# Two column strips for the band mask, two diagonal tiles for the causal mask

## What is computed

```python
def band_attention(q, k, v, mask):       # four layers
    # query chunks of W = 64 attend to 3W keys (prev/current/next chunk), band-masked
    scores = einsum('bhcqd,bhckd->bhcqk', qc, kb) / sqrt(d)
    rel = arange(3 * W)[None, :] - W - arange(W)[:, None]
    band_ok = abs(rel) <= W
    allowed = mb & pos_ok & band_ok
    scores = where(allowed, scores, -1e9)
    probs = softmax(scores)
...
def _L0_attn_ref(x, ...):                # one layer, after a layer norm
    att = einsum('bhqd,bhkd->bhqk', q, k) * D ** (-0.5)
    att = where(tril(ones((T, T))), att, -inf)
    att = softmax(att)
```

## Time and profile before

| | |
|---|---|
| median of 3 runs | 5886.05 us (5884.61 to 5886.73) |
| the profiled execution | 5917.47 us, its span 5915.7 us |
| PE busy | 5233.6 us, 88% |
| PE weight loads busy | 4004.3 us, 68% |
| DVE busy | 3505.7 us, 59% |
| ACT busy | 2533.2 us, 43% |
| POOL busy | 1121.5 us, 19% |

### The profile page before, as it was taken

One profiled execution on the slowest core, in us unless ns is written; L12 is line 12 of the kernel. 1 busy time (PEld: TensorE's weight loads), 2 busy tenths in 40 slices (PEclk: granted clock), 3 DMA queues, 4 the chain that ended last, 5 costly groups with the idle time before them and its releaser, 6 DMA issues. The chain is left out here.

```text
span 5915.7 us, 122499 instructions
## 1 busy us (share of the span) xinstructions
PE 5233.6 (88%) x43730; PEld 4004.3 (68%) x43730; DVE 3505.7 (59%) x8938; ACT 2533.2 (43%) x4800; POOL 1121.5 (19%) x1056
## 2 busy tenths in 40 slices
PE   0799998999999899999999999699999822899999
PEld 0577776777777677777777777466666622676666
DVE  6566665566666566666566666477777567222222
ACT  0355554455554455555455555255555500111111
POOL 5111111111111111111111111000000002333343
PEclk9999999999999999999999999899999956899999
DMA  6544444544444544444444444344434300323332
GB/s 100 110 87 94 88 91 78 97 96 85 94 87 85 97 84 97 84 97 85 87 95 84 97 83 88 72 88 88 90 86 93 69 9 4 93 63 78 83 81 41
DMA packets 1283995, 488.99 MB, mean 83 GB/s; under 512 B 1086531, under 2 KB 1270560, under 8 KB 1283872
## 3 DMA queue, kind: packets, MB, share of 16 engines
q1 hardware_dynamic: 1256224, 450.68, 36.0%
q0 software_dynamic: 27648, 36.72, 4.0%
HBM read 162.87 MB, written 60.28 MB: 38 GB/s over the span
## 5 line engine op out<-in xcount | busy, mean ns | idle before, releaser
L757 ACT ACTIVATE pT<-banks 128x384 f32<-128x384 f32 x1920 | 924.9, 491 | 663.6 <-PE banks L522 662.8
L965 DVE TENSOR_REDUCE mx<-banks 128x4 f32<-128x768 f32 x768 | 719.3, 950 | 304.6 <-PE banks L504 304.6
L1147 POOL TENSOR_TENSOR rstd<-ve,half 128x2 f32<-128x2 f32 x288 | 218.9, 760 | 3240.9 <-DVE ve L874 3240.9
L612 PE MATMUL banks<-nT,w 64*128 64x256 f32 x5760 | 754.2, 394 | 21.7 <-DMA b<-in_b 2.9
L502 PE MATMUL banks<-maskb,eyeb 128*128 128x384 bf16 x1920 | 633.9, 330 | 52.4 <-DMA qkT<-stack 25.2
L612 PEld LDWEIGHTS banks<-nT,w 64*128 64x128 f32 x5760 | 515.7, 187 | 191.8 <-PE banks L612 79.1
L504 PE MATMUL banks<-qkT 128*128 128x192 bf16 (+2 forms) x3840 | 634.5, 247 | 0.0
L522 PE MATMUL banks<-qkT 128*128 128x192 bf16 (+2 forms) x3840 | 633.9, 247 | 0.0
L625 PE MATMUL banks<-w,pT 128*128 128x192 f32 x3072 | 554.5, 330 | 0.0
L625 PEld LDWEIGHTS banks<-w,pT 128*128 128x128 f32 x3072 | 492.7, 190 | 42.4 <-issue 21.9
L520 PE MATMUL banks<-mseq,eyeb 128*128 128x384 bf16 x1536 | 502.7, 327 | 18.2 <-DMA qkT<-mrT 14.8
(11 more groups left out here) (200 smaller groups left out, 8602.3 us busy)
## 6 DMA issues: line engine op xcount, KB each, us to landing
hcur<-hbuf SPq DMA_DIRECT2D x164, 192.0 KB, 2.6
resid<-hbuf SPq DMA_DIRECT2D x160, 192.0 KB, 2.5
amb<-am_d SPq DMA_DIRECT2D x130, 192.0 KB, 3.1
hbuf<-hout SPq DMA_DIRECT2D x128, 192.0 KB, 2.0
exp_wg<-in_ewg SPq DMA_DIRECT2D x16, 768.0 KB
exp_wu<-in_ewu SPq DMA_DIRECT2D x16, 768.0 KB
exp_wd<-in_ewd SPq DMA_DIRECT2D x16, 576.0 KB
xs<-xr SPq DMA_DIRECT2D x32, 272.0 KB, 2.2
```

The source lines that it names most:

```text
L612: last = nc.tensor.matmul(up_bank(s, f), w1[rows, c, up_cols(ph, f)], nT[s][rows, c, :], start=(step == 0), stop=(step == 2))
L757: ph.inc(nc.scalar.activation(pT[s][:, h % NPT, :], bank[s][h % 2][:, 0:SCOLS], ACT.Exp, scale=SCALE), "p", s)
L965: last = nc.vector.tensor_reduce(mx[s][:, :, at].rearrange("p t h -> p h t"), src[:, :, 0:SCOLS].rearrange("p h (t k) -> p h t k", t=T), A ...
```

## The change

In the banded layers the mask is written by two matmuls. The first takes the identity's columns 0 to 63 and writes rows 0 to 63 of the bank, columns 64 to 383; the second takes the identity's columns 64 to 127 and writes rows 64 to 127, columns 0 to 319. Both are placed by `tile_position`, at column 0 and column 64 of the array, and the program gives them a 128 x 64 tile. What is left out (row below 64 with column below 64, row from 64 on with column from 320 on) holds no closed entry. In the causal layer one matmul writes columns 0 to 127 and 256 to 383 (a stepped output and a stepped mask operand), 256 columns in place of 384. The score matmuls still accumulate on what the mask wrote and overwrite the rest. `stop=True` and `skip_group_check=True` on them change no operation.

```diff
+        def pe_masks(ph, dst, mask):
+            if ph is tok:
+                nc.tensor.matmul(dst[0:D64, D64:SCOLS], eyeb[:, 0:D64], mask[:, D64:SCOLS], start=True, stop=True,
+                                 tile_position=(0, 0))
+                nc.tensor.matmul(dst[D64:P, 0:SCOLS - D64], eyeb[:, D64:P], mask[:, 0:SCOLS - D64], start=True,
+                                 stop=True, tile_position=(0, D64))
+            else:
+                ends = lambda x: x[:, 0:SCOLS].rearrange("p (x c) -> p x c", c=P)[:, 0:3:2, :]
+                nc.tensor.matmul(ends(dst), eyeb[:], ends(mask), start=True, stop=True)
...
-            nc.tensor.matmul(dst[:, 0:SCOLS], eyeb[:], maskb[:, masks, :], start=True, stop=False)
+            pe_masks(ph, dst, maskb[:, masks, :])
             for t, (c0, f0, w) in enumerate(qcols):
                 last = nc.tensor.matmul(dst[:, c0:c0 + w], qT[s][:, h, t * P:(t + 1) * P],
-                                        kT[s][:, h, f0:f0 + w], start=False, stop=(t == T - 1))
+                                        kT[s][:, h, f0:f0 + w], start=False, stop=True, skip_group_check=True)
...
-            nc.tensor.matmul(dst[:, 0:SCOLS], eyeb[:], mseq[s][:] if ph is tok else maskb[:, 3, :], start=True, stop=False)
+            pe_masks(ph, dst, mseq[s] if ph is tok else maskb[:, 3, :])
```

More of the change, by code:

```diff
@@ L519, in pe_scores2 @@
             dst = bank[s][h % 2]
-            nc.tensor.matmul(dst[:, 0:SCOLS], eyeb[:], mseq[s][:] if ph is tok else maskb[:, 3, :], start=True, stop=False)
+            pe_masks(ph, dst, mseq[s] if ph is tok else maskb[:, 3, :])
             for t, (c0, f0, w) in enumerate(kcols):
                 last = nc.tensor.matmul(dst[:, c0:c0 + w], kT[s][:, h, t * P:(t + 1) * P],
-                                        qT[s][:, h, f0:f0 + w], start=False, stop=(t == T - 1))
+                                        qT[s][:, h, f0:f0 + w], start=False, stop=True, skip_group_check=True)
             ph.inc(last, "sc2", s)
```

## The result

The changed kernel takes 6403.05 us (median of 4 runs, 6397.0 to 6406.7), the kernel before 5885.33 us beside it: ratio 1.088, 95% interval 1.0861 to 1.0899, 518 us slower. The forecast was 6493 us, its range 6170 to 6700.

The account below looks back on a forecast made before the run. TensorE was taken to bound the banded layers: +0.23 us a block made +642 us, +630 after absorption; the causal layer gave -20. The total, +610 on the profiled 5917.5, scaled to +607 on 5886: 6493 us, own range 6330 to 6700.

Parts of the forecast that it names:

- The bound: Banded layers: TensorE is busy 26.7 to 26.8 of a 27.00 us turn, so time added to its stream lengthens the turn.
- the late weight load: Banded strips: after a change of tile shape their weight load is not hidden, costing 0.05 us a mask (0.01 to 0.11).
- Side by side: Banded mask: both strips run together, the second starting about 0.007 us later; net saving 0.02 us a mask.
- The change of tile: Banded blocks: switching between full tile and 128*64 strips costs 0.095 us going in and 0.10 us coming out.
- The two masks after products: Two of a banded turn's 24 masks follow products, where one change stood already; they cost +0.125 us, not +0.23.
- The wait that hides 0.3 us: Banded turn: the first F block's wait for VectorE's addition (L1054) disappears behind longer K blocks, -0.3 us a turn.
- The causal layer: Causal masks of 256 columns for 384 save 0.65 us a turn, -20 us (-41 to 0); waits take back the rest.
- Free strips: Rival: 64-column banded strips need no change of tile, a mask takes 0.143 us for 0.163; 5805 us, chance 0.08.
- The clock: Rival: TensorE's granted clock falls to 1.2 GHz in the score phase; 6950 us for half the blocks, chance 0.10.
- One change only: Rival: banded masks pay only one tile change, or weights load across one; 298 us less, about 6195 us, chance 0.08.
- strips in a row: Rival: the two banded strips run one behind the other, +0.13 us a block, 400 us, 6890 us; chance 0.04.
- the changes of layer: At the three layer changes TensorE's waits for weights absorb only 12 us of the loss (0 to 30).

Follow-up runs that it names:

- e3: Changed kernel with the banded layers' score matmuls also cut into the two 64-column strips: 5848.5 us, ratio 0.9894 to the kernel before.
- e4: Changed kernel with both masks first, then both score pairs, in a banded turn's ten steps with F and K blocks: 6158.2 us, ratio 1.0419.
- e5: Changed kernel with the banded mask as four strips of 32 rows and all 384 columns instead of two of 64: 6422.5 us, ratio 1.0925.
- e7: Changed kernel with strips only in the banded K blocks, F keeping its full mask of 384: 6126.8 us, ratio 1.0419.
- e1: Changed kernel with the banded mask again one full-tile matmul, so only the causal mask is cut: 5896.5 us, ratio 0.9975.
- e6: e3 with each score strip also leaving out its one fully closed 64-column piece: 5794.7 us, ratio 0.9856.

## Why the prediction was right, and where it was off

**The bound: right.** TensorE's stream is the banded turn, before and after. In the changed kernel 0.20 us a block, 22 times, and 0.09 twice, less the 0.3 us wait, is 4.3 us, the turn's growth. The forecast of the loss was 607 us and 518 were measured, 90 too many, nearly all of it in one term (the late weight load, below).

**Side by side: right.** The second strip starts within 0.01 us of the first. I had taken 0.007 us; the median of the 3072 pairs is 0.003.

**The change of tile: right, in both directions.** In: from the last score's start to the strips, 0.176 us where scores alone are 0.083 apart, medians of the banded blocks (the 0.26 to 0.27 from the scores' first start to the strips is 0.093 + 0.176). Out: 0.26 less 0.136 of streaming and 0.024 of weights, 0.10. Rows of other shapes and formats gave the price of a shape that the trace did not have. e3 (no changes, no loss), e4 (half) and e5 (same shape as its neighbour, nothing paid) show that the change of shape is its cause. The rule of the Trainium skill that I weighed (TensorEngine Tiling, Key Properties: changing the mode, not just the tile, drains the engine) agrees with the runs in its cases: nothing between two tiles of one shape (e3), the price on the way in and out, and again from 32 to 64 columns. Whether the array drains in that time no row shows.

**The late weight load: too large, and the main miss.** It is a weight load of which a part stays uncovered after a change of shape. I took 0.05 us from the two small tiles of the earlier trace rows, interpolated by columns between their 32 and 128. e4 shows 0.02, more exactly 0.024 (0.160 from its first pair of strips to its second, less 0.136). Both rows are float32, while the strips are bf16, and I left the format out: by those rows a float32 load costs 0.02 for 32 columns, and the strips cost that for 64. e5 bears that out at one tile shape: from its last strip to the scores it is 0.269 us (median), and 0.258 where the strips stand behind products and no change of shape uncovers the load. So 32 bf16 columns lose 0.011 us where the float32 products of the same tile lose 0.02. 3072 x 0.026 = 80 us of the 90 that the forecast was too high. My lower bound, 0.01, came from a bf16 row, and I called the float32 rows nearer because of their tile. The Trainium skill's formula (TensorE: Matmul & The Clock Gate, LDWEIGHTS: columns / 1.2 ns, an estimate of 0.053 us for 64) is for the whole load. It is twice what is left uncovered here, and the measurement decides.

**The two masks after products: right in kind.** They paid +0.125 in my sum and about 0.09 in the trace, by the same smaller weight term.

**The wait that hides 0.3 us: right.** It is gone from TensorE's waits, and e7 shows it once more.

**The causal layer: right in kind, a little high.** 0.54 us a turn for 0.65. The wait on VectorE's maxima grew from 0.3 to 0.8 us, the step I had named. e1 measured 16.7 us alone for 20 forecast. The stepped output has no price of its own: a block there is 0.27 us in the changed kernel (4813.14, 4813.42 and 4813.69 below), 0.054 less than 0.33, the columns' share.

```profile
4813.14 0.27 PE L498 MATMUL banks<-maskb,eyeb 128*128 128x256 bf16 x1
4813.42 0.27 PE L498 MATMUL banks<-maskb,eyeb 128*128 128x256 bf16 x1
4813.69 0.27 PE L498 MATMUL banks<-maskb,eyeb 128*128 128x256 bf16 x1
```

**The rivals.** Free strips, 5805 us, failed, but only because of what stands between them: e3 takes away the neighbours of another shape and comes out 1.1% under the kernel before. The clock stayed at 1.00 in the steady turns, with the array streaming little more than half of a block. One change only, and strips in a row, are both excluded by the rows above.

**The scale** from the profiled execution to the median, 0.53%, was not a general stretch (last section). It moved the sum by 3 us only. The 12 us that I let the changes of layer absorb were about right (10 in the sum of the turns, 12 in their waits). My own range of 6330 to 6700 is not the sum of its bounds, which gives 6306 to 6709; nothing hangs on it.

## What to carry to other kernels

Before cutting a matmul into column strips, look at its neighbours: a strip between full-tile matmuls pays about 0.19 us for the two changes of shape, more than the 0.16 us that the whole 384-column mask took here, and 32-column and 64-column strips are different shapes. Bring the neighbours into the same shape, or gather the strips, and the price goes (0.30 us a block instead of 0.53). And when the price of something new is read from rows of something similar, match the number format too, not only the shape.

## What the runs showed of the hardware that was not expected

**Halves of the array run on their own.** In e6 one half of the array streams 128 and then 192 score columns and the other 192 and then 128. If a strip had to wait for the wider one of the pair before it, a block would stay at e3's 0.30 us; it is 0.27 to 0.28, the 640 columns of each half (320 of mask, 320 of scores) at 0.163 us for 384.

**The expert stage has two speeds.** It is the same code in all kernels. Here are 820 us of it in the profiled executions of the kernel before and of the changed one:

```profile
5060.00:5880.00 820.00, 799.38 (x3939) 568.88 (x3938) 193.30 (x338) 129.85 (x218) 295.76 (x232) 1.00 0.31 71
...
5560.00:6380.00 820.00, 810.67 (x4056) 615.00 (x4057) 198.78 (x348) 133.35 (x224) 303.12 (x239) 1.00 0.31 72
```

In the same time and at the same granted clock the second gets through 4056 matmuls, the first through 3939, 3% fewer. From the first to the last `ps_u` matmul of the stage it is 828 to 833 us in the kernel before and in e1 to e4, and 800 to 802 us in the changed kernel and in e5 to e7. That is about 30 us, the size by which the profiled execution of the kernel before lay above its median (31 us) and the kernel before ran slower beside e1 to e4 than beside e5 to e7 (33 us). e1 to e4 ran on one chip and e5 to e7 on another, so it seems to go with the chip and not with the kernel; that was not tested, and its cause stays open.
